# A megakernel of two macaron blocks: its string of steps placed anew, filler products left out

## What is computed

```python
x = x + 0.5 * int8_matmul(norm(x), weight_q, weight_scale, bias)      # L0 ffn
x = x + attn0(norm(x))          # 16 heads of width 8, rope, causal softmax, W_O
x = x + 0.5 * int8_matmul(norm(x), weight_q, weight_scale, bias)
x = x + 0.5 * (silu(n @ wg.T) * (n @ wu.T)) @ wd.T                    # n = norm(x), hidden 384
x = x + attn1(norm(x))          # 16 heads of width 64, causal softmax, w_o
x = x + 0.5 * (silu(n @ wg.T) * (n @ wu.T)) @ wd.T
```

## Time and profile before

| | us |
|---|---|
| median of 3 runs (805.39 to 808.4) | 807.03 |
| the profiled execution | 807.12 |
| its span | 805.3 |
| PE, DVE, ACT, POOL busy | 730.1, 535.3, 456.4, 466.8 |

### The profile page before, as it was taken

One profiled execution on the slowest core, in us unless ns is written; L12 is line 12 of the kernel. 1 busy time (PEld: TensorE's weight loads), 2 busy tenths in 40 slices (PEclk: granted clock), 3 DMA queues, 4 the chain that ended last, 5 costly groups with the idle time before them and its releaser, 6 DMA issues.

```text
span 805.3 us, 21573 instructions
## 1 busy us (share of the span) xinstructions
PE 730.1 (91%) x9393; PEld 433.4 (54%) x9406; DVE 535.3 (66%) x743; ACT 456.4 (57%) x535; POOL 466.8 (58%) x367
## 2 busy tenths in 40 slices
PE   2767888888888899899999999999999999999997
PEld 1633455445334544564555665555676555675764
DVE  7699966888778764777675675555537556654037
ACT  2424679976666489555635655665443665636312
POOL 6714566600750300399969577877745986667840
PEclk9755989999989999999999999999999999999999
DMA  8000000000000000000101111011001101111100
GB/s 268 2 1 2 3 2 2 3 2 2 2 2 2 2 2 2 3 2 2 28 2 29 28 30 30 3 28 28 29 2 28 29 2 28 29 29 29 28 27 27
DMA packets 13225, 16.20 MB, mean 20 GB/s; under 512 B 3052, under 2 KB 10572, under 8 KB 13132
## 3 DMA queue, kind: packets, MB, share of 16 engines
q1 hardware_dynamic: 12556, 14.50, 6.4%
q10 hardware_dynamic: 576, 0.33, 0.1%
HBM read 13.26 MB, written 1.17 MB: 18 GB/s over the span
## 4 chain that ended last, share of the span: by engine, by line
PE 72%; DVE 18%; ACT 6%; issue 3%; DMA 0%; POOL 0%; ACTq 0%; DVEq 0%
PE ps L1274 20%; PE ps L1223 17%; DVE big L1087 9%; PE ps L1194 6%; PE ps L1438 5%; PE ps L1253 5%; ACT Pr L710 4%; PE ps L1475 3%; PE ps L1443 2%; PE ps L1395 2%; PE ps L1284 2%; PE ps L1389 1%; DVE moments L1031 1%; PE ps L1264 1%; PE ps L1361 1%
## 5 line engine op out<-in xcount | busy, mean ns | idle before, releaser
L710 ACT ACTIVATE Pr<-ps,exp_scale 128x1024 f32<-128x1024 f32 (+1 forms) x283 | 278.8, 1034 | 138.4 <-PE ps L1274 73.4
L1118 DVE TENSOR_REDUCE mxb<-ps 128x8 f32<-128x1024 f32 (+1 forms) x152 | 173.9, 1165 | 89.9 <-PE ps L1274 61.0
L692 POOL TENSOR_TENSOR V0s<-V0s,Pr 128x1024 f32<-128x1024 f32 x77 | 182.1, 2366 | 61.9 <-ACT Pr L710 31.2
L1087 DVE TENSOR_REDUCE big<-ps 128x8 f32<-128x1024 f32 (+1 forms) x167 | 170.4, 1071 | 30.9 <-PE ps L1253 18.4
L1274 PE MATMUL ps<-big 64*128 64x128 f16 (+2 forms) x2560 | 169.0, 259 | 0.4 <-issue 0.3
L1253 PE MATMUL ps<-big 32*128 32x128 f16 (+2 forms) x1280 | 104.2, 280 | 38.2 <-DVE big L1087 24.3
L1274 PEld LDWEIGHTS ps<-big 64*128 64x128 f16 x2560 | 92.8, 94 | 71.5 <-issue 19.8
L1223 PE MATMUL ps<-Pr,V1s 128*64 128x128 f32 (+2 forms) x960 | 111.3, 371 | 0.0
L1253 PEld LDWEIGHTS ps<-big 32*128 32x128 f16 x1280 | 42.6, 96 | 111.7 <-ACT Pr L710 39.4
L607 POOL TENSOR_TENSOR stats<-moments 128x8 f32<-128x8 f32 x9 | 1.9, 211 | 168.3 <-DVE moments L1031 168.3
L692 POOL TENSOR_TENSOR acts<-acts,Pr 128x1024 f32<-128x1024 f32 x35 | 82.6, 2359 | 11.7 <-POOL acts L692 4.1
(11 more groups left out here) (242 smaller groups left out, 928.1 us busy)
## 6 DMA issues: line engine op xcount, KB each, us to landing
rec_b<-scratch_dram SPq DMA_DIRECT2D x30, 256.0 KB, 3.9
X<-in_x_dram SPq DMA_DIRECT2D x2, 256.0 KB, 3.4
big<-in_pick_rows_dram SPq DMA_DIRECT2D x2, 256.0 KB, 3.2
X<-in_x_dram SPq DMA_DIRECT2D x1, 512.0 KB, 6.4
rec_b<-in_w_q_dram SPq DMA_DIRECT2D x1, 512.0 KB, 6.3
XT<-in_w_k_dram SPq DMA_DIRECT2D x1, 512.0 KB, 7.1
XT<-in_w_v_dram SPq DMA_DIRECT2D x1, 512.0 KB, 7.7
wo_s<-in_w_o_dram SPq DMA_DIRECT2D x1, 512.0 KB, 8.7
```

The lines of the kernel that those rows point to most:

```text
L692: g.tensor_tensor(dst, dst, src, ALU.add).then_inc(summed, 1)
L710: ins = a.activation(dst[:, part], src, func, scale=scale)
L1087: ins = v.tensor_reduce(maxima_of(mall[:, r, 2 * u:2 * u + 2][:, part], i), block_view(src, i), AX.X, ALU.max, negate=True)
L1118: ins = v.tensor_reduce(maxima_of(mxb[:, r][:, part], arg), block_view(src, arg), AX.X, ALU.max, negate=True)
```

## The change

The string `ORDER` is another one, over the same 985 steps: each stream keeps its own order, only how they are laid together differs. The table `KEEP` is empty, so 19 filler products are gone; those of head and tail stay. And the values' product (pv) gets the two waits that pq and pk have, since it may now stand first of the three.

```diff
 ORDER = (
-    "ammmmmmmmammmmmmmmmmmmmtmmmeehmmmaememhehehwmemhwemwmememmeewmhmehwemhwemewtehmmwememewhmeaeewmhmmhm"
+    "ammmmmmmmammmmmmmmmmmhhmamtememememhwhemewmemwememwmememwehmhmehehmwwemtheeewmhememwmemwemegemwemmhm"
 ...
 KEEP = {
-    ('gmax', 1, (7, 1)): 2,
-    ('gmax', 5, (1, 0)): 1,
-    ('gexp', 4, (6, 0)): 2,
-    ('gmax', 1, (4, 0)): 1,
-    ('gexp', 5, (1, 0)): 1,
-    ('gexp', 1, (6, 1)): 1,
-    ('gmax', 1, (0, 0)): 3,
-    ('gexp', 4, (5, 1)): 1,
-    ('gmax', 6, (0, 0)): 2,
-    ('gexp', 0, (7, 0)): 1,
-    ('gmax', 6, (2, 0)): 2,
-    ('gmax', 7, (8, 0)): 1,
-    ('gmax', 6, (8, 0)): 1,
 }
...
                 if kind == "pv":
+                    pe.wait_ge(slot_dve, read("V", "xt", (4, key // NP), None))
+                    pe.wait_ge(w_split, 3)
                     x16, w16 = X1[:, key // NP], wqkv1[:, 2, :, tile(key % NP)]
```

More of the change, by code:

```diff
@@ L185 @@
 ORDER = (
-    "ammmmmmmmammmmmmmmmmmmmtmmmeehmmmaememhehehwmemhwemwmememmeewmhmehwemhwemewtehmmwememewhmeaeewmhmmhm"
-    "hewmemwememgehhhmhhemtwehmeewemewmemhehmhhehwmewmhmwmeamegemeweemwmhwemewmemmeewemmteewmememwmemwmew"
-    "memgeaemewmemwemwememmeewemewemmwemtemwemwmememwmeegmmhmmhhemhwemwmemhehwemewaeehtemwmemwemmmeheehwe"
-    "hmwemwhemhewmemememwewemewmheagemhhhhwhhewmememmhtemwehemwmememmwemhememmhewegemwemwmemwememeweeewtQ"
-    "eKweeweewMeweegMweeVMeweMewMeewMeweeVMweeMwMwgTKhQhEhMEhMWMEWMEEMWMMEWEMhhKQWVMEWTMhMEWWEMWMEMWEMWME"
-    "WhMEEhhVShhEMQKWTWEEMWMMWWMEMWMEEhEEWhhEWhhVhhEMWMQhhKShMWMEMWTEMWWMEMWWEMEWWWMEEEMWMSWThKQVWMEEEMWW"
-    "MEMWMEEEEEEMWWMMMWSQKVTWWWMEMWMEEMWWMESMEMWMMVKQTWWEEEMWMEMWEEMWWEMWWMEMWMEEEEMWWSTQKVWWMEEEEMWMWMMW"
-    "WMEEEEEMWWMEEMSKQVTWWWWMEEMWWMMWEEEKEMWWMEEMWWMMQSWWTMEEMWMMEWWEMVVOMEEEMWSMEEEMWOKOTQOMEMWWWWMMEhWW"
-    "WMEEMWMMEWMEESQKVThWWMEMWMEEMWWMEMWWMEEEEhVWSMEMWWTQhhWKEWEMEhEMWWMMMWWSMEEEEhhWWWMEEMWMhKQVTWWMEEMW"
-    "MWMEMWMEEEKWWMEMWMEQThVEMSEMMWWWMEEMWWWMEEMWWMEEEMWWWTSEEEEWWWWEEEEEESWWOOOOEEWWWWWWW"
+    "ammmmmmmmammmmmmmmmmmhhmamtememememhwhemewmemwememwmememwehmhmehehmwwemtheeewmhememwmemwemegemwemmhm"
+    "mhmewmeeemwmehamehwmmhhhtmmhmemwemewmeemeemwhmwmhmhemwhemehewemmwemegeamewemmewmemtemwemmemwmeaemhwm"
+    "emwemewemegmewewemmhwemeemtemewemewmemwhmemwemmemwemgeemwhmmmhheewehmhewmamewemhewemewemetmhemwmemwm"
+    "ememwmeewmhemheawmehmeehwewmememewmhemwemgeewmmhetwmmhhhhhheewemheewehwmeewmeemewmegeemwemhewmmhwemm"
+    "KKQtQVweMeeMwMeewMegeweMeweMeweMeweMeweMeweeTQKwwMMgEEEMWMEMWWMMWEEEEMWWhWMEMhTVhMQKWhhEMWMEEESWWMEE"
+    "MWMMWWMEEMWTWMhEQKVEWhMWMEMWMEEEMWMEMSMEMWMhTEhEVQVhKhWEWWWMMMWWEEEWMMhWWMEMWMEMWMSTEMWMEEWMMKEWWEMV"
+    "hWWEEhQTWShhWEEMMWWMEEEhhhWWQKhMEWMEMWEMMWhEEhMWEMEWMMVTSEMMWWEMMWWEVhWEEEMWWWMEESTEEQKWWMMMWWWEEMWM"
+    "EMWMEEEEMWSEMQVKTWWWMWEEEMWMMWWMEEMWQKVSWWMEEVMMWWEEMTWMEEMWWMEMWMMEWMWSEEKOQEEWEMEMEMWMWVMTOWWMMOQM"
+    "OSEMKWWEEMEhWWMEMWWETWMEEMWMWMEMWEMWMEEEhEWWKVQTSEWWEMWMEEMWMMMWWMEWMEEEKVQVWEMMWWMEEEMWWTMMSWWWEMQK"
+    "EWEMMWEMMWEEEEEhVWSTWWWWMEEMWMWEMMWWMEEEMWSEEEEMWWWWThhhWWEEEEWEEEOhOEWWWWSEOhhOhWWWW"
 )
```

## The result

| us | before | after |
|---|---|---|
| median of 4 runs each | 806.81 (805.39 to 808.4) | 793.04 (791.85 to 795.27) |
| the profiled execution | 807.12 | 794.18 |
| its span | 805.3 | 792.4 |

The changed kernel takes 0.9838 of the time, with a 95% interval of 0.9812 to 0.9864: 13.8 us less. Faster was forecast, and 793.04 lies within the range, but the gain is nearly twice the 7.3 us of the sum.

A forecast was written before the change was run, and what follows sets the result against it. PE's products bound the second attention; the first is bound by PE, DVE and ACT waiting in turn. 807.0 + 2.2 - 1 - 1.5 - 5 - 2 = 799.7 us, range 790 to 809.5.

The forecast's parts named there:

- The bound: Second attention: sum of PE's products; first attention: PE, DVE and ACT wait in turn, 39.4 us ceiling for reordering.
- Changes of the tile, +2.2: From step 399 to the string's end, 22 more array-tile changes at 0.10 us each: +2.2 us, range 0 to +2.5.
- Fillers, -1: First attention: 19 constant products go, mostly covered by waits: -1 us, bounds -7.8 and 0.
- The start, -1.5: First attention's start: third exponential comes 4.9 us earlier, near 68.5 us; a third taken: -1.5 us, range -5 to +1.
- The rest of the first attention, -5: Busier engine's load by hundreds of steps suggests -10 us; half taken beyond the start's share: -5, range -10 to +4.
- rival D: Half-speed stretch ends 7 us earlier and three slow-clock pieces vanish, 3.5 and 4.2 us gained: 792 us; chance 0.13.
- The first pairs of the second attention, -2: From 295 to 420 us, batch middle spread over more steps, shortening PE's waits: -2 us, range -4 to +2.
- The end and the new waits, 0: Last MLP moves near the string's end, still covered by weighing steps; two waits before the values' product: 0 us.
- Idle only moves (B): First attention keeps its 39.4 us idle, gives 0 to 2 us: 803 to 810, middle 806; chance 0.27.
- The clock falls more often (C): Without fillers at 13 places, more 3.4 us half-speed pieces at 1.4 us each; eight make 811 us; chance 0.15.
- It doesn't do what it says: Whole string: tile changes rise instead of falling, costing 0.3 to 2.2 us; counted within the unchanged-time case, no own chance.

The follow-up runs named there:

- new to 200: Changed string up to step 200, then the remaining steps in the old order, no fillers, against the kernel before: 811.62 us, ratio 1.0062.
- the single third hundred: Old string to step 200, changed order to step 300, old order behind it, no fillers, against the kernel before: 811.73 us, ratio 1.006.
- regrouped from 700 on: Changed string to step 700, old order behind it, weighing steps moved next to steps of their tile, against the changed kernel: 804.0 us.
- both regroupings: Changed kernel with weighing steps moved beside steps of their tile, either from step 484 on (809.0 us) or with old order from step 700 (804.0 us).
- new to 600: Changed string up to step 600, then the remaining steps in the old order, against the changed kernel: 820.34 us, ratio 1.0162 to the kernel before.

## Why the prediction was right, and where its sum was off

**The bound.** Right: the second attention is the sum of PE's products (350.70 of 351 us), and the gain came mostly from the first.

**Changes of the tile, +2.2.** Right: +2.3 over the string, of which 22 more behind the first key product, as counted; the price held up when it was taken 216 times.

**Fillers, -1.** Nothing in the old string (1.001), 1.8 to 3.3 us in the new one, both within the bounds of 0 and 7.8. What I had not seen is that it may depend on the string. A reason would be that products which waits had covered stand in PE's way where it waits less; no run shows that by itself.

**The start, -1.5.** The mechanism was right, and its time to under a microsecond. ACT's order of time after, beside the earlier trace rows:

```profile
67.02 3.36 ACT L697 ACTIVATE Pr<-ps,exp_scale 128x1024 f32<-128x1024 f32 x3 [3.66 <-PE ps L1231]
70.92 1.11 ACT L697 ACTIVATE Pr<-ps,exp_scale 128x1024 f32<-128x1024 f32 x1 [0.54 <-PE ps L1240]
```

The third exponential begins near 69.2 us (forecast 68.5 to 69, before 73.40). The first hundred gives 2.3 us, with the same 44.4 us at half clock, fillers included; -1.5 and a share of the fillers' -1 were forecast.

**The rest of the first attention, -5.** The forecast of where the gain would lie failed in the second hundred and in the third, and that these errors cancelled in part was luck. By the stretches the order alone is worth +3.7 - 6.4 + 0.3 = -2.4 us there; by the comparison at equal mean clock it can be some 2 us more. I had taken the busier engine's load by hundreds, said that the second hundred shows the gain best, and that the third loses only one dequantisation. By this cut of the string the second hundred became 3.7 us longer, as DVE's load rose from 43.95 to 50.03 us in it, past the 47.48 us of ACT that had been the fuller. The gain shows in the third, where DVE has 5.9 us less to do and idles 4.4 us less. Halving the -10 was too kind by up to 2.6 us, and still within -10 to +4.

**The clock, which had no term.** Here lies half or more of the missing 5.6 us (12.9 of spans against 7.3), by either way of splitting. The sum was made as if the half clock stayed, and the fewer pieces stood beside it as rival D, to which the sum's gain was not added back as a case of its own: D was priced as one of two ways to go, at 0.13, while both happened. With the new order came less half clock, and less half clock is worth 0.2 to 0.4 us per us. That it came because PE waits less is not shown: PE's idle in the first attention fell by 2.6 us only. From 112 us on 20.4 us at half clock became 6.8, while the long stretch's 6.8 us less came back at 92 us. D's price for a piece, 1.4 us of 3.4, was at the upper end of what was measured (0.2 to 0.4 us per us, 0.7 to 1.4 for a piece), and its result of 792 is near the measured 793, though not by its parts: it wanted 3.5 us from the first stretch, which came to nothing (44.4 us at half clock in both first hundreds), and 4.2 from the pieces, which gave 2.8 to 4.9.

**The first pairs of the second attention, -2.** Low by half. The waits behind the first key product fell by 4.1 us. L1353's 0.96 us is gone: its line (L1340) starts at 385.9 us after a pause of 0.2. Up to the first exponential PE is idle 0.6 instead of 1.7 us, up to 410 us 0.8 instead of 3.6 up to 420. By steps, what is left over fell by 5.0 us up to step 600 and rose by 1.0 behind it; 1.1 us of products had moved ahead of the first key product, and 2.0 went into the changes: 4.1 + 1.1 - 2.0 = 3.2 of the 3.3 us. The reason, spreading, is supported by what bunching costs (11.9 us at one place), not shown for this place by itself.

**The end and the new waits, 0.** Right. The string's last steps on PE run without a gap into the sum:

```profile
759.82 1.15 PE L1210 MATMUL ps<-Pr,V1s 128*64 128x128 f32 x18
760.90 1.07 PE L1271 MATMUL ps<-V0s,ones_s 128*32 128x512 f32 x8
762.69 0.66 PE L1483 MATMUL ps<-id_s,big 128*128 128x128 f32 x4 [0.72 <-ACT big L862]
```

**The rivals.** *Idle only moves (B)* is refuted for the whole string by its own test (idle of the first attention: DVE 42.1 to 34.1 us, ACT 86.5 to 75.2). For the pieces it can hold: new to 200 and the single third hundred gained nothing. *The clock falls more often (C)* is refuted; without fillers the profiled execution of the old string had more of it (77.5 against 64.9 us), as C had said of fillers, but the medians over executions are 76 and 72 us, and the time was the same. The Trainium skill (TensorE: Matmul & The Clock Gate, "A second HAM failure mode: psum-queue depth-cycling") ties such swings to short idles between groups of products. The traces agree in that the pieces came where PE's waits were short (at most 1.2 us for DVE). They don't show that fewer such idles mean less half clock: with the new order the third hundred had none with PE idle for 5.5 us of it, and 10.2 us with PE idle for 5.7 (regrouped from 700 on). *It doesn't do what it says* was right as to the count, and cost what was said.

**The sum again**, profiled: order of the first attention -4.7, half clock -4.9, second attention -3.3 gives -12.9 us, which is the difference of the spans. The first two share 9.6 us; how they share it stays open by some 2 us (-6.8 and -2.8 by the comparison at equal mean clock).

## What to carry to other kernels

Where three engines wait for each other in turn, judge an order by the whole stretch: the load that one part takes on can be relief for the next, and a piece taken alone (new to 200, the third hundred) showed a loss where the whole gained. Give the clock a term of its own in the sum, here 3 to 5 of 13 us, and compare many executions before you price it; and take a change of tile for a fixed price that is worth paying where it covers waits for another engine, as both regroupings showed.

## What the runs showed of the hardware

- A change of the array's tile costs 0.09 to 0.10 us and nothing hides it on a full PE: 216 more, with 144 products of 16 columns, made 21.5 us.
- The time at 1.2 GHz is not fixed by the program: ten executions of one kernel had 58 to 92 us of it (from mean clocks of 0.964 to 0.943) and spans of 799.9 to 810.2 us. It is nearly all of the spread of that kernel's times (correlation 0.98). A line through the executions gives 0.21 to 0.35 us for each us, by kernel, and stretches of the profiles 0.24 to 0.40: less than the half that PE alone would lose. That part of such time is waiting for DVE anyway would explain it; it was not tested.
- PE fell to the lower clock for 20.5 us in the midst of the second attention (new to 600): for 6.8 us from 441.2 us on, within a wait of 2.9 us that followed one of 2.5, and for 13.7 us from 454.8 us on, within a wait of 11.9; in the changed kernel, which has no wait of 2 us there, it stays at 2.4 GHz from 242.4 us to the string's end.
